# Causal mask of the diagonal blocks added by TensorE, row maxima by plain reductions over whole banks

## The reference

```python
qkv = x @ w_attn + b_attn                      # 4 x 512 x 768
q, k = rope(q), rope(k)                        # 16 heads of 16 channels
scores = einsum('bhtd,bhsd->bhts', q, k)       # 512 x 512 a head
scores = where(tril, scores, -inf)
attn = softmax(scores, axis=-1) * E ** -0.5
o = einsum('bhts,bhsd->bhtd', attn, v)
x = layernorm(x + o @ w_proj + b_proj)
x = layernorm(x + experts(x))                  # router, top 2 of 8
```

## Time and profile before

| what | us |
|---|---|
| median of 3 runs | 625.55 |
| the 3 runs | 621.55, 625.55, 629.4 |
| span of the profiled execution, first to last instruction | 614.3 |
| what lies around the span, against the median and against the lowest run | 11.3 and 7.3 |

### The profile page before, as it was taken

How to read it: one execution, slowest core, us unless ns; L and a number is a source line. 1 busy time by engine, 2 the same in 40 slices (tenths; PEclk the granted TensorE clock), 3 DMA queues, 4 the chain that set the end, 5 groups by cost and what they waited for, 6 DMA issues and landing times.

```text
span 614.3 us, 11017 instructions
## 1 busy us (share of the span) xinstructions
PE 459.8 (75%) x2891; PEld 273.0 (44%) x2892; DVE 296.7 (48%) x957; ACT 272.3 (44%) x385; POOL 207.0 (34%) x344
## 2 busy tenths in 40 slices
PE   5799699999948988787402998878888788787700
PEld 4364145555425544454400565545555455454400
DVE  3575988878835797647881222212222122122105
ACT  0368257757854787579352232222222222222205
POOL 2100121321351135226252253443444434434323
PEclk9799579999988999899755999999999999999955
DMA  8258775646492547030101123222232232322237
GB/s 274 41 188 249 228 286 177 198 151 199 131 51 72 181 142 52 0 104 2 44 25 26 27 44 43 34 44 41 43 43 34 43 43 34 47 39 43 43 67 233
DMA packets 52366, 57.86 MB, mean 94 GB/s; under 512 B 13040, under 2 KB 47856, under 8 KB 50784
## 3 DMA queue, kind: packets, MB, share of 16 engines
q1 hardware_dynamic: 36624, 39.91, 24.0%
q0 software_dynamic: 8688, 10.83, 10.8%
q10 hardware_dynamic: 7024, 6.77, 3.6%
HBM read 39.49 MB, written 18.16 MB: 94 GB/s over the span
## 4 chain that ended last, share of the span: by engine, by line
PE 24%; DMA 18%; issue 15%; POOL 15%; DVE 13%; SPq 6%; ACT 5%; another core or an unknown queue 1%; POOLq 1%; ACTq 0%; DVEq 0%
DMA IDX<-slot_token 10%; POOL sum_rows L1130 9%; PE PS L948 5%; PE PS L909 5%; DVE PS L719 5%; POOL PT L1120 3%; SPq L1097 3%; PE PS L930 2%; PE PS L380 2%; DMA Q<-qk_parts 2%; PE PS L983 2%; PE PS L1226 2%; SPq L464 2%; DMA W<-w_attn 1%
## 5 line engine op out<-in xcount | busy, mean ns | idle before, releaser
L719 DVE CUSTOM_DVE_ANT_0 PS<-PS,CB 128x512 f32<-128x512 f32 (+3 forms) x256 | 121.0, 514 | 45.6 <-PE PS L909 34.5
L1226 PE MATMUL PS<-W,PT 128*128 x468 | 116.1, 385 | 3.5 <-issue 2.7
L598 ACT ACTIVATE PT<-PS 128x1024 f32<-128x1024 f32 x80 | 80.7, 1023 | 56.8 <-PE PS L931 46.1
L1196 DVE SCALAR_TENSOR_TENSOR PT<-PS,CW,PT 128x512 f32<-128x512 f32 x39 | 29.3, 751 | 142.4 <-PE PS L1226 142.4
L1120 POOL DMA_INDIRECT PT<-x_rows,IDX x42 | 41.6, 989 | 141.1 <-DMA IDX<-slot_token 140.5
L909 PE MATMUL PS<-K,Q 96*128 96x512 bf16 (+3 forms) x256 | 66.5, 326 | 26.8 <-DVE MX L719 21.8
L1247 PE MATMUL PS<-W,PT 128*128 x312 | 74.8, 383 | 2.2 <-DVE PT L1199 0.9
L1160 ACT ACTIVATE PT<-PS 128x512 f16<-128x512 f16 x40 | 23.9, 597 | 110.6 <-PE PS L1217 110.6
L1130 POOL DMA_INDIRECT sum_rows<-PT,IDW x39 | 62.1, 1592 | 18.9 <-issue 11.3
L1247 PEld LDWEIGHTS PS<-W,PT 128*128 128x128 f32 x312 | 58.5, 190 | 17.3 <-issue 7.3
L1226 PEld LDWEIGHTS PS<-W,PT 128*128 128x128 f16 x468 | 45.7, 98 | 42.0 <-issue 8.9
(11 more groups left out here) (141 smaller groups left out, 672.6 us busy)
## 6 DMA issues: line engine op xcount, KB each, us to landing
W<-w1T SPq DMA_DIRECT2D x8, 1024.0 KB, 5.7
qk_parts<-W SPq DMA_DIRECT2D x16, 384.0 KB, 3.4
K<-qk_parts SPq DMA_DIRECT2D x96, 64.0 KB, 2.4
Q<-qk_parts SPq DMA_DIRECT2D x96, 64.0 KB, 2.4
W<-w2T SPq DMA_DIRECT2D x4, 1024.0 KB, 5.0
W<-xT SPq DMA_DIRECT2D x4, 512.0 KB, 10.2
x_rows<-X1S ACTq DMA_DIRECT2D x4, 512.0 KB, 3.0
sum_rows<-X ACTq DMA_DIRECT2D x4, 512.0 KB, 5.5
```

What stands on the lines that cost most here:

```text
L598: act.activation(PT[n][:, :], STb[slot_of(k, n)].rearrange("p a n -> p (a n)"), ACT.Exp).then_inc(s["exp"], 1)
L719: last = dve.tensor_tensor_reduce(src, src, maskS[:, TT * P - w:], 1.0, LOW, ALU.add, ALU.max, MX[p][:, h, i:i + 1])
L1196: dve.scalar_tensor_tensor(HH, U, CW[:, :], SIL, ALU.mult, ALU.mult).then_inc(f["h"], 1)
L1226: last = mm(dst, XGT[q][:, x_part, k, :], w1h[:, bass.ds(at, UNIT)], start=(k == x_part == w_part == 0), stop=(k == KC - 1 and x_part == 1))
```

## The change

Granules are cut anew: 11 a unit in place of 10, each of one row block only. Granules 0 to 3 are row block 3 of one head (512 columns), 4 to 7 row block 2 of one head (384), 8 and 9 row block 1 of two heads (2 x 256), and granule 10 is row block 0 of all four heads (4 x 128). TensorE adds the mask: behind each matmul of scores a second one, identity times the 128 columns of `maskS`, accumulates on the diagonal block. VectorE takes the maxima of a whole granule by one `tensor_reduce`, without mask and without writing the bank: 11 instructions a unit in place of 32. Since 11 is odd, the bank of a granule is now counted through the four units.

```diff
-NSG, NTG = 10, 5
+NSG, NTG = 11, 5
...
-        maskS = CB[:, 4 * P:8 * P]
+        maskS = CB[:, 7 * P:8 * P]
...
             if n < 4:
-                return ((n, 3, 0),)
+                return 3, (n,)
             if n < 8:
-                return (n - 4, 2, 0), (n - 4, 0, 3 * P)
-            return (2 * (n - 8), 1, 0), (2 * (n - 8) + 1, 1, 2 * P)
+                return 2, (n - 4,)
+            if n < 10:
+                return 1, (2 * (n - 8), 2 * (n - 8) + 1)
+            return 0, tuple(range(GH))
...
-                for h, i, at in granule(n):
-                    w = (i + 1) * P
-                    src = Sb[n % 2][:, at:at + w]
-                    last = dve.tensor_tensor_reduce(src, src, maskS[:, TT * P - w:], 1.0, LOW, ALU.add, ALU.max, MX[p][:, h, i:i + 1])
-                last.then_inc(s["Sf"], 1)
+                i, heads = granule(n)
+                w = (i + 1) * P
+                src = Sb[(k * NSG + n) % 2][:, 0:len(heads) * w]
+                dve.tensor_reduce(MX[p][:, heads[0]:heads[0] + len(heads), i], src.rearrange("p (h s) -> p h s", s=w), AX.X, ALU.max).then_inc(s["Sf"], 1)
...
-                dst = Sb[n % 2]
-
-                for h, i, at in granule(n):
-                    w = (i + 1) * P
-                    last = mm(dst[:, at:at + w], Q[p][0:SK, h, i * P:(i + 1) * P], K[p][0:SK, h, 0:w], start=True, stop=True)
+                dst = Sb[(k * NSG + n) % 2]
+
+                i, heads = granule(n)
+                w = (i + 1) * P
+                for m, h in enumerate(heads):
+                    mm(dst[:, m * w:(m + 1) * w], Q[p][0:SK, h, i * P:(i + 1) * P], K[p][0:SK, h, 0:w], start=True, stop=False)
+                    last = mm(dst[:, m * w + i * P:(m + 1) * w], identb, maskS, start=False, stop=True)
                 last.then_inc(s["S"], 1)
```

## The result

| | us, median | runs | ratio to before, 95% interval |
|---|---|---|---|
| before | 624.16 | 621.55 to 629.4 | |
| changed | 635.32 | 633.99 to 640.78 | 1.018, 1.0123 to 1.0238 |
| changed, measured once more | 631.31 | 629.11 to 637.32 | 1.0137, 1.0085 to 1.0188 |

The change makes the kernel slower by 7 to 11 us, 1.4 to 1.8%, and both intervals leave out no change. The forecast was 628.9, 3.3 us more than before; the direction was right and the size a third to a half of what came.

The account below looks back on a forecast made before the run. It took the chain of waits to bound a plain unit, about three quarters on TensorE, a quarter on VectorE. Plain units +1.3, units 0 and 1 +1.0, units 6 to 15 +1.0 made +3.3: 628.9 us, range 615 to 639.

Parts of the forecast that it names:

- rival E: Slower: nothing is given back, as a reduction takes as long as the present pair; 13.3 us more, 638.9; chance 5%.
- What bounds the kernel: Plain unit of attention: the chain of waits decides, 7.49 us on TensorE and 2.28 on VectorE, 9.77 in all.
- The 11.3 us around the span: Whole kernel: time outside the profiled execution's span of 614.3 us, its time taken as the median of 625.55.
- TensorE's added work: Each unit: 16 mask matmuls of 128 columns at 0.055 us, 0.88 us more; TensorE's stretch goes from 7.49 to 8.37.
- Rival D: Slower: weight loads of short matmuls show, each costing 99 ns and not 55; 11.3 us in all, 640.2; chance 6%.
- VectorE's saved work: Plain reductions of 0.69 and 0.56 us; the VectorE stretch of a plain unit falls from 2.28 to 1.73.
- the 40 that were named as a sign: Sign: VectorE's busy time in attention falls by some 40 us or more without the time following.
- The plain unit: Units 2 to 5: from 9.77 to 8.37 + 1.73 = 10.10 us, +0.33 each, +1.3 in all.
- Units 6 to 15: Ten units with layernorm or routing: +0.1 us each, between -0.4 and +0.5, +1.0 in all.
- Units 0 and 1: First two units at half clock: +1.0 us for the two; -1.5 if TensorE's clock rose earlier.
- Rival C: The 9.11 us hole at 173.97 goes as VectorE's program gets shorter: 617.3; chance 12%. Mirror, one more hole: 640.5, 4%.
- B: VectorE holds more than the chain shows and the whole saving arrives: 10.1 us less, 615.5; chance 9%.

Follow-up runs that it names:

- masks alone: Kernel before, with one mask matmul added behind each of its 16 score matmuls and VectorE left as it was: 638.01 us, ratio 1.0216.
- reductions alone: Changed kernel without the mask matmuls of its maxima, 11 granules and 11 plain reductions kept: 623.39 us, ratio 0.9991.
- the two profiles with plain stores: Changed kernel and kernel before, each with the loop's 16 indirect scatters replaced by plain stores: 607.82 us (0.9753) and 600.26 us (0.9666).
- ten granules with plain reductions: Kernel before with its ten granules, each of 16 operations with mask and accumulator read replaced by one plain reduction without mask: 609.68 us, ratio 0.9849.

## Why the prediction came out as it did

The forecast had the direction and, in the main, the mechanism right: more work for the engine that most of a unit hangs on. Two terms of its sum were too small, one was too large. That 635.32 us lies within 615 to 639 is luck in part. The units account for 5 to 8 us of the 11.2, the rest is of the size by which the holes vary, and the range reached so far up for rival E, which didn't happen.

**What bounds the kernel** was right. TensorE holds a plain unit altogether now, and the two parts measured apart (masks alone 0.72 a plain unit more, reductions alone 0.28 less) have the signs and nearly the sizes of the working. The 11.3 us around the span were not there (1.8 to 1.9 in all runs that tell); the sum is a difference, so it didn't suffer.

**TensorE's added work**, 0.88 us a unit, measures 0.84 (10.27 less 9.43 of the earlier trace rows) and 0.90 in the run with masks alone. The loads of the identity are covered. Rival D is out: 0.90 / 16 is 56 ns. The Trainium skill's figure of about 81 ns (TensorE: Matmul & The Clock Gate, Back-to-back issue gap) does not hold at this place; the measurement decides.

**VectorE's saved work.** Means of 0.686 and 0.552 us for 0.69 and 0.56, and a stretch of 1.70 for 1.73 in the run without masks. TensorE's waits for the reductions fell from 21.8 to 10.5 us, half as forecast, but 8.3 of the 21.8 stood in the hole. VectorE's busy time fell by 16.7 us in all and not by the 40 that were named as a sign; that figure doesn't follow from the prediction's own 7.70 less 7.07 a unit, which makes 10.1.

**The plain unit is the first term that was too small.** I added 8.37 and 1.73 to 10.10 us and let TensorE's own work in the second stretch go, because "it stood idle 0.34 and 0.45 us there". Those two idle times were of rows of weight loads, PEld, and not of matmuls. The matmuls' own table had the bound: 9.43 busy plus 0.88 is 10.31, more than 10.10, and 10.27 came. What TensorE had to spare in a unit was 0.34 us, not 0.79. The row for it was the first that I had read and put aside as exaggerated by overlap. In the chain after, the first stretch (96.56 to 105.02) is 8.46 us for 8.37, and the second (to 106.82), now TensorE's, 1.80 for 1.73. The term is +0.50 instead of +0.33.

**Units 6 to 15** were the larger miss in sum. I put +0.1 on each for what VectorE's stretches there would return. The steps from unit 6 to 7, 7 to 8, 8 to 9 and from 5 to 6 grew by 0.18, 0.42, 0.51 and 0.81, some 0.5 on average. In the two profiles with plain stores the ten steps from 5 to 6 up to 14 to 15 grew by 5.1 us in all. So there too TensorE's stream seems to set most of the length, which no run tests by itself. Only where `post` and `normal_rows` stand does the faster VectorE return it: the steps from 6 to 7, 10 to 11 and 14 to 15 change by +0.18, -0.37 and -0.18 in that pair.

**Units 0 and 1** at half clock: +1.0 forecast, and 15.71 became 16.05, +0.3, with the time up to unit 2's PV about unchanged (22.49 and 22.39 us). The clock didn't rise within them: their rows have a granted 0.50, as before.

Free of holes the difference is 7.6 us by the medians and 5.5 by the spans, against +3.3. By the profiles the three plain steps grew by 0.50 each, the ten behind them by 5.1 in all, and the step from 15 to 16 shrank by 1.45, for a reason that wasn't looked for.

**The holes.** Rival C took the 9.11 us of before for something of VectorE's program that may fall elsewhere. The place was right and the mechanism was not: the scatters are a condition, and the kernels with them at this place have such holes in both rounds of the loop in six of eight profiles. The one that the prediction read has a single one. The difference between 7.6 and the 11.2 of the first measurement (6.9 of the second) is of the size by which they vary. B and E are out: neither did the whole saving arrive, nor was nothing given back.

**Open.** Why TensorE's signals reach the others late while GpSimd scatters was not settled, nor why ten granules with plain reductions lose half as much by it. The runs show that the indirect stores are needed for it and that they aren't enough: one unit later, three kernels have no such hole in the chain, and wait for GpSimd instead. A better time that rests on this (609.68) may not last through another edit. Not tried was to put `inverse_std` ahead of the late scatters, which would test that wait.

## What to carry to other kernels

When an edit moves work from one engine to another, add the work to the receiving engine's own busy time in one period and compare with the period: 9.43 + 0.88 against 9.77 gave the answer that the chain of waits, followed, missed by a third. Idle time of weight-load rows is no idle time of TensorE. The mask in the maximum was not needed at all: softmax takes any upper bound as its shift, as long as the exponentials don't vanish. To leave it out beat adding it on TensorE by 8 to 10 us. Against adding it on VectorE it gained 0.2 to 0.3 us a plain unit, which shows in the whole with ten granules (609.68 us) and not with eleven (623.39 for 623.54). And a step that grows elsewhere when work is moved isn't proof that the same wait moved: the chain names what stands there now.

## What the runs showed of the hardware

While 8 indirect stores of 128 slots of 8 bytes ran from GpSimd, VectorE went on up to 12.7 us late on semaphores raised by matmuls, and ScalarE 9.3; the stores cost some 23 us in all in either kernel. Plain stores of the same bytes from the same queue to fixed rows did none of this: 600.26 us for 623.54. With the indirect stores one unit later (625.08 us) no wait of this kind is left in the chain. One of them comes every 1.27 us from GpSimd (at 253.06, 254.33 and 255.60 there), and what stands behind them in its program waits. TensorE's granted clock fell to half within each long hole, in which TensorE stood idle for up to 10 us, and stayed there for a while behind it; one PV at half clock takes 1.94 us for 1.06.
